# Segment attention re-tiled: scores and output product by row halves, keys and queries projected alike, values turned through DRAM, exponentials taken straight from PSUM

## The reference

```
H, DK, DV, SEG, D = 16, 64, 64, 128, 256
q = (x @ Wq.T).reshape(B, n_seg, H, SEG, DK)      # k and v alike
for each segment (mem and z start at 0):
    sq = elu(q) + 1 ; sk = elu(k) + 1
    z  += sk.sum(over positions)
    scores  = q @ k.T / 8                          # 128 x 128 for each head
    att_dot = softmax(scores) @ v
    att_mem = (sq @ mem) / (sq @ z)
    mem += sk.T @ v
    att = gate * att_mem + (1 - gate) * att_dot    # gate = sigmoid(betas)
    y   = att.reshape(B, SEG, H * DV) @ Wout.T
```

## Time and profile before

| | us |
|---|---|
| median of 3 runs | 2681.51 (2674.93 to 2712.87) |
| the profiled execution's own time | 2676.68 |
| its span, first to last instruction | 2674.9 |
| TensorE busy | 2322.2 (87%) |
| VectorE busy | 1800.2 (67%) |
| ScalarE busy | 1315.9 (49%) |
| GpSimd busy | 664.2 (25%) |
| mean granted TensorE clock | 0.958 of full speed |

### The profile page before, as it was taken

The page is one execution under the profiler, slowest core; times in us unless marked ns, Lnnn a source line. Parts: engine busy times, 40 slices in busy tenths (PEclk is TensorE's granted clock), DMA queues, the critical chain, the costliest instruction groups (busy, mean ns, idle before and its releaser), DMA issues. The chain is left out here.

```text
span 2674.9 us, 40313 instructions
## 1 busy us (share of the span) xinstructions
PE 2322.2 (87%) x15480; PEld 1582.6 (59%) x15480; DVE 1800.2 (67%) x2865; ACT 1315.9 (49%) x2786; POOL 664.2 (25%) x673
## 2 busy tenths in 40 slices
PE   4889998888888998838999889699999997559998
PEld 4677777777777777725666645334444442336666
DVE  6655555555555555567888677777777772588885
ACT  1666566566665666523333123156666666333332
POOL 0232222222222222221222023311111112622211
PEclk9999999999999999978999899789999999979999
DMA  5000000000000000020000012533333300100000
GB/s 177 1 1 1 1 1 1 1 1 2 1 1 1 1 1 1 1 94 0 1 1 1 1 59 83 119 49 50 50 49 54 57 13 7 33 0 16 14 15 20
DMA packets 47470, 65.70 MB, mean 25 GB/s; under 512 B 6912, under 2 KB 32384, under 8 KB 47120
## 3 DMA queue, kind: packets, MB, share of 16 engines
q1 hardware_dynamic: 40384, 53.15, 9.2%
q10 hardware_dynamic: 6864, 9.91, 1.0%
q0 software_dynamic: 32, 0.07, 0.0%
HBM read 46.06 MB, written 17.04 MB: 24 GB/s over the span
## 5 line engine op out<-in xcount | busy, mean ns | idle before, releaser
L1599 ACT ACTIVATE PT<-PSUM 128x512 f32<-128x512 f32 (+3 forms) x768 | 332.2, 495 | 202.4 <-PE PSUM L1572 197.3
L1630 DVE TENSOR_REDUCE MXP<-PSUM 128x1 f32<-128x640 f32 (+6 forms) x352 | 349.5, 1026 | 109.8 <-PE PSUM L1533 108.3
L1531 PE MATMUL PSUM<-kS,qS 96*128 96x512 bf16 (+3 forms) x768 | 204.8, 344 | 36.4 <-DMA kS<-k_parts 18.1
L762 POOL TENSOR_TENSOR EX<-EX,RC 128x512 f32<-128x512 f32 x128 | 133.2, 1041 | 346.3 <-DVE RC L698 346.3
L1572 PE MATMUL PSUM<-qS,kS 98*128 98x512 bf16 (+3 forms) x768 | 207.9, 330 | 9.0 <-ACT PT L1599 8.8
L740 DVE TENSOR_TENSOR DG<-PSUM,MODR 128x256 f32<-128x256 f32 x32 | 12.1, 419 | 273.8 <-PE PSUM L534 273.8
L1676 POOL TENSOR_SCALAR_AFFINE_SELECT PT<-PT 128x512 f32<-128x512 f32 x128 | 81.4, 636 | 444.1 <-ACT PT L1599 444.1
L1155 POOL TENSOR_TENSOR FHQ<-FAH,FSH 128x704 f32<-128x704 f32 x64 | 88.3, 1401 | 387.0 <-DVE FAH L798 387.0
L896 PE MATMUL PSUM<-FWG,FXQT 128*128 128x352 f32 x512 | 169.3, 475 | 5.0 <-ACT FXQT L966 2.7
L896 PE MATMUL PSUM<-FWU,FXQT 128*128 128x352 f32 x512 | 166.2, 468 | 6.2 <-DVE FHH L1068 6.1
L1548 PE MATMUL PSUM<-PT,VB 128*32 128x512 f32 (+3 forms) x1536 | 163.6, 498 | 1.4 <-POOL PT L1676 0.6
(11 more groups left out here) (212 smaller groups left out, 5208.9 us busy)
## 6 DMA issues: line engine op xcount, KB each, us to landing
qS<-q_parts SPq DMA_DIRECT2D x96, 128.0 KB, 4.2
kS<-k_parts SPq DMA_DIRECT2D x96, 128.0 KB, 6.4
q_parts<-PARTS SPq DMA_DIRECT2D x16, 384.0 KB, 2.8
k_parts<-PARTS SPq DMA_DIRECT2D x16, 384.0 KB, 2.8
out_x<-X SPq DMA_DIRECT2D x16, 256.0 KB, 2.1
X<-in_x ACTq DMA_DIRECT2D x4, 512.0 KB, 10.2
X<-in_x SPq DMA_DIRECT2D x4, 512.0 KB, 9.6
WM<-in_wmod SPq DMA_DIRECT2D x2, 768.0 KB, 12.4
```

Of the source, the lines that this page charges most:

```text
L762: pool.tensor_tensor(EX[:, gr % NEX, :, :], EX[:, gr % NEX, :, :], RC[:, 4 * gr:4 * gr + 4].unsqueeze(2).to_broadcast([128, 4, 128]), ALU. ...
L1531: mm = pe.matmul(ps[:, b, c0:c0 + width], ST["q"][gr % 4][0:96, h, t * 128:(t + 1) * 128], ST["k"][gr % 4][0:96, h, k0:k0 + width], start= ...
L1599: act.activation(PT[at % 2][:, h, 0:N], SB[u % 3][:, 0:N], ACT.Exp, scale=CAUSAL_SCALE).then_inc(s_e, 1)
L1630: dve.tensor_reduce(MXP[:, gr % 2, heads[0]:heads[-1] + 1, t], src, AXX, ALU.max, negate=True).then_inc(s_mx, 1)
```

## The change

Only what computes layer 0's attention changes; the arithmetic is the same up to the order of sums.

- Keys and queries are projected by one function, 64-column weights per block and batch half, so a bank holds a batch in each partition half. Keys are stored in order of position (`KTR`, one plain tile), queries in the order block, token. `split_pairs`, `KB` and `VT` go.
- Scores: two matmuls per head, one on rows 0 to 63 and one on rows 64 to 127, into two banks (banks 0 and 1 alone); eight matmuls for four heads at a time ("q"), at steps -1, 1, 3, 5.
- One VectorE maximum over both banks (128 x 1024); no subtraction: ScalarE takes exp from PSUM with the maximum as bias, in pieces of 128 x 128, and 1/8 is folded into the copy of the queries.
- Values: tokens as rows (weights `HT`, 512 channels streamed), copied to `VN`, written to DRAM and read back by SP in pieces of 256 B; the transposes and the copy of "tv" go. GpSimd's gate multiplication is 4 instructions of 128 x 512.
- The attention output is copied by one instruction per bank into `ATT` (in `QT`'s room), and the output product contracts 64 rows per batch with a 64-row copy of `Wout` in each partition half (loaded twice). It runs in the next iteration, behind its keys.
- "qs" goes through the four 32-column groups in turn; "sl" contracts 32 rows. The banks are handed out least recently used first, and within the steps among banks 2 to 5 save for the scores.

```diff
+class Banks:
+    def take(self, key, sem, value, among=None):
+        at = min(among or self.banks, key=lambda b: self.last[b])
...
-            act.dma_start(W0["o"][:, :, :], A["wo0"].rearrange("(t p) n -> p t n", p=128)).then_inc(g.w_in, 16)
+            for half in range(2):
+                act.dma_start(W0["o"][64 * half:64 * half + 64, :, :], A["wo0"].rearrange("(c v) n -> v c n", v=64)).then_inc(g.w_in, 16)
...
-        work_at = {0: [("mm", 0)], 1: [("mm", 1), ("mm", 2), ("ht", 0)], 2: [("mm", 3), ("qs", 0), ("pv", 0)], 3: [("sl", 0)],
-                   4: [("mp", 0), ("sl", 1), ("pv", 1)], 5: [("mp", 1), ("sl", 2)], 6: [("sl", 3)], 7: [("pv", 2)], 9: [("pv", 3)]}
+        work_at = {-1: [("mm", 0), ("mm", 1)], 0: [("mm", 2), ("mm", 3), ("pv", 0)], 1: [("qs", 0), ("pv", 1)], 2: [("pv", 2)], 3: [("sl", 0), ("sl", 1)],
+                   4: [("mp", 0), ("mp", 1)], 5: [("sl", 2), ("sl", 3)], 6: [("pv", 3)]}
...
+                        turns.take(("qk", it, 2 * q + half), s_ex, it * 8 + 2 * q + 2, [half])
...
+                for it in range(NIT):                       # SP
+                    if it:
+                        sp.wait_ge(s_vin, 32 * it)
+                    for n in range(4):
+                        sp.wait_ge(s_pvc, it * 4 + n + 1)
+                        sp.dma_start(VD[n // 2, :, n % 2 * 512:n % 2 * 512 + 512], VN[:, n % 2, :]).then_inc(s_vst[n % 2], 16)
+                    if it:
+                        sp.wait_ge(s_mm, it * 4)
+                        sp.wait_ge(s_vg, it * 4)
+                    for n in range(2):
+                        sp.wait_ge(s_vst[n], 32 * (it + 1))
+                    for half in range(2):
+                        sp.dma_start(V[:, :, half, 0:DK], VD[half].rearrange("a n -> (a n)").rearrange("(h p v) -> p h v", p=128, v=DK)).then_inc(s_vin, 16)
...
+                    for ci in range(4):                     # project, keys and queries
+                        c = 4 * n + ci
+                        for half in range(2):
+                            for k in range(KT):
+                                mm = pe.matmul(view[64 * half:64 * half + 64, ci, :, :], W[w][:, k, c * DK:(c + 1) * DK], HT[:, k, half, :], ...)
+                def project_rows(it, n):
+                    for k in range(KT):
+                        mm = pe.matmul(ps[:, :], HT[:, k, n // 2, :], W["v"][:, k, n % 2 * 512:n % 2 * 512 + 512], ...)
...
-                    for n in range(2):
-                        mm = pe.matmul(ps[:, n * 256:(n + 1) * 256], QT[:, 2 * gr + n, :], KB[:, 2 * gr + n, :, :].rearrange("p a k -> p (a k)"), start=True, stop=True)
+                    for hh in range(4):
+                        for half in range(2):
+                            sl = slice(64 * half, 64 * half + 64)
+                            mm = pe.matmul(ps[half][:, hh * 128:(hh + 1) * 128], QT[sl, 4 * q + hh, :], KTR[sl, 4 * q + hh, :], start=True, stop=True)
...
+                def products(it):
+                    ps = [take("y", it, half) for half in range(2)]
+                    pe.wait_ge(s_oc, it * 4 + 4)
+                    for c in range(16):
+                        for half in range(2):
+                            sl = slice(64 * half, 64 * half + 64)
+                            mm = pe.matmul(ps[half][:, 0:D], ATT[sl, c, :], WO[sl, c, :], start=(c == 0), stop=(c == 15))
...
                 for it in range(NIT):                       # TensorE
+                    for n in range(4):
+                        project("k", "pk", it, n, s_pk)
+                    if it:
+                        products(it - 1)
...
+                    for n in range(4):
+                        project("q", "pq", it, n, s_pq)
+                    if it + 1 < NIT:
+                        turn_x(it)
+                    for step in range(-1, 13):
...
+                        if step in (-1, 1, 3, 5):
+                            scores(it, (step + 1) // 2)
...
-                            act.activation(EX[:, step % NEX, :, :], EX[:, step % NEX, :, :], ACT.Exp, scale=SEG_SCALE).then_inc(s_ex, 1)
+                            for hh in range(2):             # two heads x two batches of a step
+                                for half in range(2):
+                                    ...
+                                    done = act.activation(EX[:, step % NEX, n, :], bank("qk", it, step // 2 * 2 + half)[:, col * 128:(col + 1) * 128], ACT.Exp, bias=MX[...])
...
+                        if step in (0, 2, 4, 6):            # VectorE
+                            dve.wait_ge(s_qk, it * 4 + q + 1)
+                            dve.tensor_reduce(MX[:, 8 * q:8 * q + 8]..., g.PSUM[:, at:at + 2, :]..., AXX, ALU.max, negate=True).then_inc(s_mx, 1)
...
+                    pool.wait_ge(s_vin, 32 * (it + 1))      # GpSimd
...
+                    for gr in range(2):
+                        for half in range(2):
+                            pool.tensor_tensor(VG[:, 8 * gr:8 * gr + 8, half, :], V[:, 8 * gr:8 * gr + 8, half, 0:DK], GR[:, 8 * gr:8 * gr + 8, :], ALU.mult).then_inc(s_vg, 1)
+                    if it:
+                        add(it - 1)
```

More of the change, by code:

```diff
@@ L55, in take, with __init__ @@
         self.freed[at] = (sem, value)
+class Banks:
+    def __init__(self, banks):
+        self.banks, self.n, self.freed, self.of = list(banks), 0, {}, {}
+        self.last = {b: b - len(self.banks) for b in self.banks}
+    def take(self, key, sem, value, among=None):
+        at = min(among or self.banks, key=lambda b: self.last[b])
+        self.last[at] = self.n
+        self.n += 1
+        self.of[key] = at, self.freed.get(at)
+        self.freed[at] = (sem, value)
 class Shared:
@@ L408, in turn_x, with project @@
                     mm.then_inc(s_xt, 1)
-                def project_pairs(w, kind, it, n, signal):
+                def project(w, kind, it, n, signal):
                     ps = take(kind, it, n)
[L412 to L416, removed]
-                    mm.then_inc(signal, 1)
@@ L419, in scores @@
-                def scores(it, gr):
-                    ps = take("qk", it, gr)
-                    if gr == 0:
+                    view = ps[:, :].rearrange("p (h t c) -> p c h t", h=NH, c=4) if w == "k" else ps[:, :].rearrange("p (h c t) -> p c h t", h=NH, c=4)
+                    for ci in range(4):
+                        c = 4 * n + ci
+                        for half in range(2):
+                            for k in range(KT):
+                                mm = pe.matmul(view[64 * half:64 * half + 64, ci, :, :], W[w][:, k, c * DK:(c + 1) * DK], HT[:, k, half, :],
+                                               start=(k == 0), stop=(k == KT - 1))
@@ new lines, in project, with scores @@
+                    mm.then_inc(signal, 1)
+                def project_rows(it, n):
+                    ps = take("pv", it, n)
+                    pe.wait_ge(s_ht, it + 2)
+                    for k in range(KT):
+                        mm = pe.matmul(ps[:, :], HT[:, k, n // 2, :], W["v"][:, k, n % 2 * 512:n % 2 * 512 + 512], start=(k == 0), stop=(k == KT - 1))
+                    mm.then_inc(s_pv, 1)
+                def scores(it, q):
+                    ps = [take("qk", it, 2 * q + half) for half in range(2)]
+                    if q == 0:
@@ L529, in _ @@
                             mm.then_inc(s_am, 1)
-                    ps = take("y", it, 0)
-                    pe.wait_ge(s_oc, it * 4 + 4)
-                    for half in range(2):
-                        for c in range(8):
-                            mm = pe.matmul(ps[:, half * D:(half + 1) * D], ATTT[:, half, c, :], WO[:, c, :], start=(c == 0), stop=(c == 7))
-                    mm.then_inc(s_y, 1)
+                products(NIT - 1)
             @block.scalar
@@ new lines, in _ @@
+                    if it + 1 < NIT:
+                        columns(it)
+                    for step in range(-1, 13):
+                        if 0 <= step < 8:
+                            for hh in range(2):
+                                for half in range(2):
+                                    n, col = 2 * half + hh, 2 * (step % 2) + hh
+                                    if n == 0 and step % 2 == 0:
+                                        act.wait_ge(s_mx, it * 4 + step // 2 + 1)
+                                    done = act.activation(EX[:, step % NEX, n, :], bank("qk", it, step // 2 * 2 + half)[:, col * 128:(col + 1) * 128], ACT.Exp,
+                                                          bias=MX[:, 8 * (step // 2) + 4 * half + col:8 * (step // 2) + 4 * half + col + 1])
+                            done.then_inc(s_ex, 1)
@@ new lines, in _ @@
+                        dve.scalar_tensor_tensor(sq, src, 0.0, sq, ALU.max, ALU.add).then_inc(s_pqs, 1)
+                    for step in range(-1, 13):
+                        if step in (0, 2, 4, 6):
+                            q = step // 2
+                            at = turns.of["qk", it, 2 * q][0]
```

(3 more changed lines are left out.)

271 lines of the change are left out of this document (105 added, 166 removed).

## The result

The changed kernel takes 2532.07 us (median of 4, 2530.51 to 2537.23); the kernel before took 2697.19 in the runs beside it. The ratio is 0.942 with a 95% interval of 0.933 to 0.951. Like with like, the profiled executions took 2676.68 and 2530.51 us: 146 us less, 5.5% faster.

The account below looks back on a forecast made before the run. TensorE's own work was taken to bound the kernel: 61.1 - 2.0 - 3.5 - 1.4 + 0.8 = 55 us per iteration, 60.5 with waits against 67.97; 16 iterations give -121.6 from 2676.7, so 2555 us, range 2530 to 2590.

Parts of the forecast that it names:

- Scores -3.5, product nothing, by row halves side by side: TensorE's row halves overlap as column halves do: scores 7.1 to 3.5 us an iteration, output product the same 7.1.
- Transposes -2.0: TensorE's 16 transposes of the values go, saving 2.0 us an iteration.
- denominators -1.4: TensorE's 32 denominator records, 2.5 us, run four at once in 1.1 us with the start of a block.
- keys written in steps of 16 B nothing: Keys going to PSUM in 16 B steps cost nothing; rival of half speed +7.1 us an iteration, chance 0.05.
- The lists walked in order: Each engine's instructions timed in order from the start of the keys: TensorE done at 59.7 us of an iteration.
- the 60.5 us for an iteration: The walk's 59.7 us plus 0.8 for switches, against 67.97 before, with TensorE idle about 5.5.
- A step's four exps: ScalarE's exps of 128 x 128 from PSUM, taken at 0.34 us each, 1.4 for four.
- the 0.8 for switches: Some 8 more changes of matmul shape on TensorE per iteration, at 0.1 us each.
- The rival of the longer chain: Exps with bias cost 0.471 us each, delaying the score banks: 64.5 us an iteration, 2619 us; chance 0.14.
- Values: Trip through DRAM costs nothing: read back takes 25 us at most, covered by keys, output product and queries.
- The product's move: Output product behind the next keys: its 2.41 us wait for ScalarE's last copies is covered by the keys.
- First iteration: VectorE still inverts the gates until 74.8 us, so first scores come at 25.9 instead of 25.1: +0.8 us.

Follow-up runs that it names:

- product_in_turn: Changed kernel with the output product issued as 16 matmuls on rows 0 to 63, then 16 on rows 64 to 127: 2632.91 us, an iteration of 65.05.
- sums_in_turn: Changed kernel with the denominators' sixteen 32-column matmuls going through the four column groups one after the other: median 2571.94 us, an iteration of 60.29.
- scores in turn: Changed kernel with the eight score matmuls of a q issued four on rows 0 to 63, then four on rows 64 to 127: 2556.71 us, an iteration of 60.50.
- product_at_end: Changed kernel with the output product back at the end of its own iteration on TensorE: 2593.30 us, iterations of 62.19 and 63.81.
- three_orders: Changed kernel with VectorE's normalization, moments, sums, maximum and denominator chain and a ScalarE value copy reordered: 2543.85 to 2545.51 us in three runs, 2577 to 2581 in three.
- subtract_first: Changed kernel with VectorE again subtracting the maximum and ScalarE taking one 128 x 512 exp in place: 2585.12 us, 61.72 an iteration at full clock.
- reads_doubled: Changed kernel with each of the two reads of the values from DRAM done twice: 2530.61 us, an iteration of 58.90.
- vector_order: Changed kernel with VectorE's normalization and moments later, fifth sum and fourth maximum earlier: 2521.98 and 2523.45 us, twice 2558; an iteration of 58.25.

## Why the prediction was right

- **TensorE sets the pace.** Its work per iteration came out at 55.15 us for 55. `product_in_turn` and `sums_in_turn` show it directly: 6.14 and 1.4 us more in a block are 6.15 and 1.39 more in the iteration.
- **Scores -3.5, product nothing, by row halves side by side.** Right: blocks of 1.16 us and 7.18 us, and both grow when the halves stand in turn. Taking the column halves as the nearest row held; no row of before could show it.
- **Transposes -2.0, denominators -1.4, keys written in steps of 16 B nothing.** The "tv" block is gone, the denominators take 1.08 us as against 2.5 in the earlier trace rows, the keys 7.26 as in the earlier trace rows. No run puts the value transposes or the four-copy taking apart back, so their shares stand by the rows alone. Shares of single edits don't add up either: 1.6 (scores in turn), 1.4, 2.8 and 3.3 are already the whole 9.1 us, before the transposes.
- **The lists walked in order.** From the start of the keys the walk had scores at 25.1, 31.8, 38.9 and 45.0; the trace has 25.5, 32.5, 38.5 and 44.5: 0.4 and 0.7 late, then 0.4 and 0.5 early, so errors of both signs cancel in it. It had the fourth maximum at 47.7, late behind VectorE's list; the trace has 47.9. The last memory product was to end at 59.7 and ended at 58.9.
- **What was off: the 60.5 us for an iteration, 1.6 too long.** The measured 58.90 lies just under the forecast's own 59 to 62.7, and the 2532 us just inside its 2530 to 2590. The last output product was forecast at 1033 and starts at 1009.96: 16 times 1.6 is 25.6 us, and 0.5 more came at the last spacing, but the first iteration and a later start gave back 3.0. That is 23.1 of the 24.6 us between 2555 and 2530.5; the rest is that product itself, 8.83 us in the earlier trace rows, at a granted clock of 0.81, and 7.18 now. TensorE's work was forecast well; its waits were not, 5.5 us for 3.75. Two terms of the sum were mis-sized. A step's four exps take 1.14 us and not 1.4: the last ones end at 52.8 instead of 53.4, and all behind them follow 0.8 earlier. And the 0.8 for switches was put on top of the walk, though the walk had waits of TensorE that can take it up; it belongs to the work (55 with it, 55.15 measured), not to the path. That is argued from the two sums, no run tests it. The rival of the longer chain, at 0.471 an exp, went the wrong way altogether.
- **Values.** Covered, as forecast; a read lands in 5.3 us where the upper end was 25. The mean packet of the earlier trace rows was a poor bound for pieces of 256 B: 4096 of them in two reads landed in about 6.5 us.
- **The product's move** was reasoned with the one wait it covers, 2.41 before. `product_at_end` shows that it covers two, 0.78 and 2.40, and that the second appears only in the new order.
- **First iteration.** +3.2 instead of +0.8: the transposes behind VectorE's late start ran at 3.49 us for 1.97, at the lower clock, and VectorE's steps of 0.43 took 0.68 and more. One iteration of 16.

## What to carry to other kernels

Where one engine is busy nine tenths of a stage, price its list by the block, then walk the other engines' lists in their order until the end of the iteration; an allowance belongs to the work or to the path, and on the path only where nothing waits. Moving a block from the end of an iteration behind the first block of the next one covers its own wait and also the wait that followed that first block, and the second was the larger. Once the waits are each about a microsecond or less, reordering other engines gives back less than it promises: 0.65 us of 1.5 here, and a loss in the next try.

## What the runs showed of the hardware

- Matmuls on different row halves (64 rows contracted, 128 weight columns, different PSUM banks) run side by side: 7.18 us against 13.32 for 64 records of 256 columns. To do so they had to be issued alternately.
- **TensorE's clock fell now and then in the kernels with more waiting, but not behind every such wait.** In `product_at_end` a wait of 2.40 us stands in every iteration, and 6 of the 14 iterations after the first have 1.2 GHz behind it, each time 10.5 to 11.0 us after the start of the keys: queries in 8.19 us for 7.26, an iteration of 63.81 for 62.19. In `three_orders` waits of 0.88 and 0.67 us within 2 us have behind them the score block of 2.08 us shown above, and an iteration later the same waits have behind them one of 1.16:

```profile
700.80 0.38 PE L546 MATMUL PSUM<-RP,SEL 32*128 32x128 bf16 x4 [0.89 <-DVE RP L727]
701.85 0.39 PE L546 MATMUL PSUM<-RP,SEL 32*128 32x128 bf16 x4 [0.67 <-ACT PT L646]
...
702.97 1.16 PE L481 MATMUL PSUM<-KTR,QT 64*128 64x128 f32 x16
```

  There 8 of 14 iterations were granted less than 1.00, each time from 38.7 to 40.3 us after the start of the keys, in `subtract_first` 12 of 14. The changed kernel, with 3.75 us of waits spread out, has none of it in 14 iterations; before, two of 15 spacings were 69.5 for 67.97. The fixed places, right behind the waits, speak for them as a cause; what more decides whether the clock falls is not shown.
- **35 us that no edit touches.** Some executions of most kernels here are longer by about 35 us (none of four of `reads_doubled` and of `product_in_turn`). The stretch is in the last feed-forward. 146.8 us of it in two executions of the same changed kernel, of 2530.5 and 2566 us:

```profile
2111.00:2257.80 146.80, 80.33 (x317) 55.44 (x318) 94.80 (x177) 45.15 (x105) 62.29 (x72) 0.79 0.05 18
```

```profile
2113.00:2259.80 146.80, 87.89 (x228) 59.06 (x228) 64.69 (x139) 34.38 (x90) 56.97 (x68) 0.50 0.06 18
```

  In the one TensorE is granted 0.79 of full speed on average and does 317 matmul records, in the other 1.2 GHz throughout and 228. VectorE's instructions, taken in order, are 0.2 us later in the longer execution at 2041 us and 35.2 us later at 2230. The traces of `sums_in_turn`, `vector_order` and `three_orders` have the same 146.8 us at 1.2 GHz there. What decides between the two was not tried.
